# Softplus of a router: Ln on ScalarE against a series on VectorE, with a new order of all engines

## The reference

```python
logits = jnp.einsum('btd,ed->bte', X, routing_W) + expert_bias
activation = jnp.sqrt(jax.nn.softplus(logits))
top_vals, top_idx = jax.lax.top_k(activation, K)      # K = 2 of E = 8
combine = jnp.sum(jax.nn.one_hot(top_idx, E) * top_vals[..., None], axis=-2)
...
routed = jnp.einsum('ne,end->nd', cf, y)              # cf: combine, y: the experts' outputs
```

## Time and profile before

| | us |
|---|---|
| three runs | 233.58, 234.48, 235.31 |
| median | 234.48 |
| profiled execution | 234.76 |
| its span, first to last instruction | 233.0 |
| mean granted TensorE clock | 0.993 |

### The profile page before, as it was taken

One profiled execution on the slowest core, in us unless ns is written; L12 is line 12 of the kernel. 1 busy time (PEld: TensorE's weight loads), 2 busy tenths in 40 slices (PEclk: granted clock), 3 DMA queues, 4 the chain that ended last, 5 costly groups with the idle time before them and its releaser, 6 DMA issues.

```text
span 233.0 us, 5313 instructions
## 1 busy us (share of the span) xinstructions
PE 222.0 (95%) x2010; PEld 158.9 (68%) x2010; DVE 175.5 (75%) x507; ACT 132.9 (57%) x292; POOL 34.7 (15%) x55
## 2 busy tenths in 40 slices
PE   7999899999999999789899999999999989899995
PEld 6422685657786797455567766767677788798495
DVE  2476544999974699998887789999889767735672
ACT  2204462346377456889998888799987731133030
POOL 2020001032214126302040230020001031210000
PEclk9999999999999999999998999999999999999999
DMA  6999959600000000007000430000007999300001
GB/s 198 402 422 450 421 236 228 136 0 0 0 4 0 3 0 1 0 17 166 3 0 4 104 82 0 3 3 1 3 3 264 429 408 414 159 0 3 0 3 45
DMA packets 2905, 26.88 MB, mean 115 GB/s; under 512 B 448, under 2 KB 704, under 8 KB 1344
## 3 DMA queue, kind: packets, MB, share of 16 engines
q1 hardware_dynamic: 2880, 26.54, 31.5%
HBM read 26.28 MB, written 0.26 MB: 114 GB/s over the span
## 4 chain that ended last, share of the span: by engine, by line
PE 72%; DVE 10%; DMA 9%; ACT 3%; issue 2%; SPq 2%; POOL 0%; DVEq 0%
PE bank L1419 11%; DMA late_sb<-late 9%; PE bank L1435 6%; PE bank L1295 6%; PE bank L1405 5%; PE bank L1238 4%; PE bank L1234 3%; PE bank L1273 3%; DVE ctx_sb L954 2%; PE bank L1218 2%; PE bank L1378 2%; PE bank L1649 2%; PE bank L1361 2%; PE bank L1537 2%; PE bank L1640 2%
## 5 line engine op out<-in xcount | busy, mean ns | idle before, releaser
L579 ACT ACTIVATE ctx_sb<-ctx_sb,small_sb 128x512 f32<-128x512 f32 x64 | 45.9, 720 | 3.0 <-DVE small_sb L954 2.7
L954 DVE CUSTOM_DVE_ANT_0 ctx_sb<-bank,mask_sb 128x512 f32<-128x512 f32 x64 | 41.9, 679 | 2.6 <-PE bank L1419 1.8
L1419 PE MATMUL bank<-early_sb,ctx_sb 128*128 128x128 f32 x256 | 36.6, 281 | 2.3 <-DVE work_sb L965 1.4
L1419 PEld LDWEIGHTS bank<-early_sb,ctx_sb 128*128 128x128 f32 x256 | 28.3, 142 | 15.2 <-ACT ctx_sb L579 8.3
L381 POOL TENSOR_TENSOR rstd_sb<-veps_sb,minus_half_sb 128x2 f32<-128x2 f32 (+1 forms) x15 | 11.0, 733 | 129.9 <-DVE veps_sb L674 129.9
L590 ACT COPY work_sb<-bank 128x512 f32<-128x512 f32 x40 | 22.8, 579 | 8.1 <-PE bank L1419 7.7
L1405 PE MATMUL bank<-k_sb,work_sb 32*128 32x512 f32 x128 | 18.2, 638 | 1.3 <-DVE small_sb L954 1.1
L722 DVE SCALAR_TENSOR_TENSOR work_sb<-bank,early_sb,work_sb 128x512 f32<-128x512 f32 x16 | 11.8, 747 | 8.3 <-PE bank L1273 7.9
L1238 PEld LDWEIGHTS bank<-late_sb,ctx_sb 128*128 128x128 f32 x128 | 15.4, 191 | 3.4 <-issue 3.3
L1435 PE MATMUL bank<-work_sb,v_sb 128*32 128x128 f32 x512 | 17.3, 275 | 0.0
L965 DVE COPY work_sb<-bank 128x512 f32<-128x512 f32 x24 | 16.4, 682 | 0.8 <-PE bank L1419 0.8
(11 more groups left out here) (264 smaller groups left out, 398.4 us busy)
## 6 DMA issues: line engine op xcount, KB each, us to landing
k_sb<-moe_w SPq DMA_DIRECT2D x1, 4096.0 KB, 12.4
ctx_sb<-moe_w SPq DMA_DIRECT2D x1, 4096.0 KB, 17.1
ctx_sb<-ctx SPq DMA_DIRECT2D x3, 1024.0 KB, 14.7
late_sb<-late SPq DMA_DIRECT2D x1, 2966.5 KB, 21.1
mask_sb<-ctx_tok SPq DMA_DIRECT2D x1, 2048.0 KB, 13.2
v_sb<-ctx_tok SPq DMA_DIRECT2D x1, 2048.0 KB, 27.1
mask_sb<-mask SPq DMA_DIRECT2D x4, 512.0 KB, 7.8
mask_sb<-mask SPq DMA_DIRECT2D x8, 256.0 KB, 4.4
```

What stands on the lines that cost most here:

```text
L579: s.activation(sc[u % NSC], sc[u % NSC], ACT.Exp, bias=smin[:, u:u + 1], scale=-1.0, accum_out=rsum[:, u:u + 1]).then_inc(sig("p1_ready"), 1)
L954: v.tensor_tensor_reduce(sc[u % NSC], bank[SB[u % GROUPS]][:, :], mask[:, KEYS * b:KEYS * (b + 1)], MASK_BIG, 3e38, ALU.add, ALU.min, smin ...
L1419: last = nc.tensor.transpose(bank[TB[u % 2]][:, P * k:P * (k + 1)], sc[u % NSC][:, P * k:P * (k + 1)], wt("ident"))
```

## The change

Softplus is computed as max(x, 0) + 2 atanh(e / (2 + e)), since ln(1 + e) = 2 atanh(e/(2+e)). With ratio r = e/(2+e), at most 1/3, and r squared, the series r (1 + r2/3 + r4/5 + ... + r16/17) is evaluated from the inside out on DVE. ACT's Ln, its wait and its signal go, and so does the test for w = 1. The number of yields in the block on DVE stays 9; on ACT it is one less per half. The strings of all four engines are new. The new line is longer in letters as each stream is called three times more often than before in the string, which adds empty calls; the set of real steps is otherwise the same, apart from G, 39 before and 34 after.

```diff
--- before.py
+++ after.py
@@ -67,25 +67,26 @@
 
 TURNS = {
     "PE": (
-        "L2 P L11 P5 L P L8 P L2 a L2 P L a P L a3 L P L P L3 P6 a P L P2 L2 a L2 a P L2 a L2 a L a P a b P "
-        "a4 b P2 b P b a P a P2 S P2 S T5 S T V b T3 S T2 V T b2 S T3 b T S b V2 b T b S b T2 P b T b2 T S T2 "
-        "V T b T b T2 V S T3 V T2 S T V c T2 S T2 c T V T2 S T2 V T S c T P T c T2 V T c S T a T V c T2 c S "
-        "T2 c T2 c V T2 c S c b T2 V T V S T c T2 c V d c d2 G T G3 c d2 G d L2 d G3 a G d2 c G d c d G9 V G2 "
-        "b G d c d G d4 G3 d G3 d c G d G d G d G V G3 c G3 d6 S d5 T d10 "),
+        "L P L P L11 P5 L P L11 a L2 P L2 a L2 a3 P L P2 L P6 L a P L P L P L a L a L2 P a L2 a L a P2 b a3 L "
+        "a2 b P2 b P2 a b a P2 S P2 T S T2 S T3 a2 b T2 V T S T b a T b V T b T S T b T2 V T S b V T2 P b S b "
+        "T2 b3 T S T2 V b T2 b T V T S T2 V T2 S T2 V T L c T2 S T c b T V T2 S T c T V S T2 c a T2 V a c T2 "
+        "S V c T2 c T2 c T S T2 c V S T c T c S T L T V T2 V c T2 L c V d c V d2 c d2 G b V d2 G d2 G S G2 d "
+        "G3 d c2 G6 d c d G d3 c G d G2 V G T S T G d V G c T G d G d2 G b G3 d G P G P G c G3 b G d9 P d2 S "
+        "d2 V c2 d S d L d7 T d2 T b P "),
     "DVE": (
-        "L18 a L a L4 a L3 a4 L a L2 a4 L a4 L a2 L2 a4 L2 a3 L a L2 P a3 L a L2 a L b L2 P a5 L a2 b a3 L a5 "
-        "P a2 b P a b3 a b a2 b a b a b2 P a b4 P a2 b2 P b S4 b2 P b S2 T b L S2 b2 S b T S b S2 b T b2 S T "
-        "S b S2 b2 S b2 T b S3 b5 S2 b T b2 a S b2 V S b4 S V T S2 V S b2 P T b2 V S b S T S b2 S T c S3 T c "
-        "S c2 T c S3 V b S V T V2 c S2 T S c S c2 T c2 S4 T c2 S T S c S c S T c S2 T S c V S c V2 S T V c S "
-        "T S c S c2 T S2 c3 S c S T c V d V d b T d2 V d V2 P V3 d8 c2 d2 c S d c d5 S c d6 c3 L d c9 V c d14 "
-        "T d4 c d7 c d3 V d3 a d2 T d8 "),
+        "L21 a L a L4 a L a3 L a L a L2 a10 L2 a3 L a L a2 L3 a2 P L a2 L a2 L P L a L2 a4 b a L b L a5 P a5 "
+        "b2 a2 P a2 b3 a2 b a b2 a b P a b P b2 a b a L b2 P b S4 b2 P S3 b S b T b L b a S b T S b3 S b S T "
+        "b a S3 T b2 S b5 T b S b S b S b2 S b2 T S2 b V P V S2 a b2 V T b2 S4 V T b4 S2 b T S2 b2 T c3 S2 T "
+        "S2 c2 T S2 T S b V S V3 T c S3 c4 S T c2 S4 T c T S2 c2 S2 c T S3 P c V T c S V2 T c V S L S3 c T c "
+        "S c T S c S c3 S2 T c a V P d3 P T V d2 V a V5 d b d4 T d3 c d c2 d3 L d T d2 c d b P d V c T d5 c2 "
+        "L c d V c9 d2 S2 V d3 S d5 T c d6 b c d3 V d S b d4 c2 d2 V d2 c d5 c T d11 "),
     "ACT": (
-        "L2 P2 L P4 a L8 P2 L a2 P a2 P a P a2 P3 L P4 L2 a L2 a2 L a L a2 L2 a2 P L2 a P b P b2 a P b2 P b2 "
-        "S P S3 P T S T2 S3 T S T S T S3 a T S b T S2 b3 T S b2 S2 T b3 a T S T S3 T S4 T2 L S b T S4 T2 S2 "
-        "T2 S2 T S T S2 T S T S T S3 T S T S c T S2 T S2 T S c b c3 S T S T2 S3 T2 S4 T S T2 S3 T c T S c4 P "
-        "c d c S d c b d5 c T2 d6 c d4 "),
+        "L2 P3 L P4 a L P L8 a3 P2 a4 P4 L P3 L P L a L2 a2 L2 a2 L2 a P a L a P b P b2 a P b4 P S P S T S T "
+        "S4 T S T2 S L S2 T S b T S2 b2 T S b S b T S b S T b L S2 T b T S2 L S2 T S3 T2 S2 b T S3 T b T2 S2 "
+        "T S T S2 P T S T S a P S2 T2 S2 T S3 P T c b S P T S2 a T2 S2 c T c2 b c S3 P T2 S b T S T S4 T S T2 "
+        "S2 T b S c S2 a T2 c3 L T c L S c T a d c d c T c2 d5 S c d3 c d a d S d7 T c d "),
     "POOL": (
-        "L a L a4 b a L a2 b a3 b a b10 c2 L b c d c d a c d a c d2 c d2 ")}
+        "a L2 a6 b a L b a3 b2 a b7 a2 b c3 L3 b2 a d a c d c d2 b2 c2 d3 b d L c d2 a c2 ")}
 
 
 
@@ -554,9 +555,6 @@
                 act.wait_ge(sig("abs_ready"), h + 1)
                 s.activation(fr[2], fr[1], ACT.Exp, scale=-1.0).then_inc(sig("e_ready"), 1)
                 yield
-                act.wait_ge(sig("w_ready"), h + 1)
-                s.activation(fr[4], fr[3], ACT.Ln).then_inc(sig("ln_ready"), 1)
-                yield
                 hidden(4, B[0:H0, HTOK:], 1)
                 yield
                 for n in range(4):
@@ -859,7 +857,7 @@
                 normalize(h, x3, tiles)
                 yield
                 e3 = lambda a: a.rearrange("p (t e) -> p t e", e=E0)
-                logit, mag, ex, wl, lw, sp, av, t0, t1, cf = fr
+                logit, mag, ex, ratio, square, sp, av, t0, t1, cf = fr
                 if h:
                     dve.wait_ge(sig("cfT_ps"), 1)
                 dve.wait_ge(sig("route_ps"), h + 1)
@@ -869,29 +867,36 @@
                 ch.join()
                 v.scalar_tensor_tensor(mag, logit, -1.0, logit, ALU.mult, ALU.max).then_inc(sig("abs_ready"), 1)
                 yield
+                ch.add(v.tensor_scalar(sp, logit, 0.0, None, ALU.max))
                 dve.wait_ge(sig("e_ready"), h + 1)
-                v.tensor_scalar(wl, ex, 1.0, None, ALU.add).then_inc(sig("w_ready"), 1)
-                yield
-                dve.wait_ge(sig("w_ready"), h + 1)
-
-                ch.add(v.tensor_scalar(t0, wl, -1.0, 1e-30, ALU.add, ALU.max))
+                ch.add(v.tensor_scalar(t0, ex, 2.0, None, ALU.add))
                 yield
                 ch.join()
                 ch.add(v.reciprocal(t0, t0))
                 yield
                 ch.join()
-                ch.add(v.scalar_tensor_tensor(t1, wl, 1.0, ex, ALU.is_equal, ALU.mult))
-                ch.add(v.tensor_tensor(t0, t0, ex, ALU.mult))
-                yield
-                ch.join()
-                dve.wait_ge(sig("ln_ready"), h + 1)
-                ch.add(v.tensor_tensor(t0, t0, lw, ALU.mult))
-                yield
-                ch.join()
-                ch.add(v.tensor_tensor(t0, t0, t1, ALU.add))
-                yield
-                ch.join()
-                v.scalar_tensor_tensor(sp, logit, 0.0, t0, ALU.max, ALU.add).then_inc(sig("softplus_ready"), 1)
+                ch.add(v.tensor_tensor(ratio, ex, t0, ALU.mult))
+                ch.join()
+                ch.add(v.tensor_tensor(square, ratio, ratio, ALU.mult))
+                yield
+                ch.join()
+                ch.add(v.tensor_scalar(t0, square, 1.0 / 17, None, ALU.mult))
+                for n in (15, 13):
+                    ch.join()
+                    ch.add(v.scalar_tensor_tensor(t0, t0, 1.0 / n, square, ALU.add, ALU.mult))
+                yield
+                for n in (11, 9, 7):
+                    ch.join()
+                    ch.add(v.scalar_tensor_tensor(t0, t0, 1.0 / n, square, ALU.add, ALU.mult))
+                yield
+                for n in (5, 3):
+                    ch.join()
+                    ch.add(v.scalar_tensor_tensor(t0, t0, 1.0 / n, square, ALU.add, ALU.mult))
+                yield
+                ch.join()
+                ch.add(v.scalar_tensor_tensor(t0, t0, 1.0, ratio, ALU.add, ALU.mult))
+                ch.join()
+                v.scalar_tensor_tensor(sp, t0, 2.0, sp, ALU.mult, ALU.add).then_inc(sig("softplus_ready"), 1)
                 yield
                 dve.wait_ge(sig("softplus_ready"), h + 1)
```

## The result

The changed kernel takes 237.07 us (median of 12 runs, 235.84 to 241.82) where the kernel before, in the same comparison, takes 234.26: ratio 1.0117, 95% interval 1.0084 to 1.0150. Medians are over all executions, while ratios and intervals leave out those over 1.5% above the kernel's fastest (here 241.55 and 241.82 of the changed one). The prediction was 233.1, at most 235.3. It was wrong in sign.

A forecast was written before the change was run, and what follows sets the result against it. PE, busy 222.0 of 233.0 us, was taken as the bound, so its holes decide. 234.76 - 0.7 (start) + 0.3 (first half) - 1.0 (second half) + 0 (tail) = 233.4; less 0.28, 233.1 us, range 230.7 to 235.3.

The forecast's parts named there:

- The rows on ACT and DVE: Busy times: ACT loses 3 table loads and 2 Ln, 4.3 us; DVE gains 14 instructions of 0.17, to near 177.9.
- The start, -0.7: Widenings on DVE ahead of the first small-stage step close PE's 0.75 hole before 27.56: -0.7 us, ends -1.3 and 0.
- only a wait for the DMA would be a new hole, 0 to 0.5: At the start, PE's first projection, now ahead of the first transposes, may wait 0 to 0.5 us for ctx.
- First half, +0.3: Softplus near 67 comes 2.1 us later, with 1.7 of cover ahead of L1353: +0.3 us, ends 0 and +1.0.
- Second half, -1.0: Softplus near 113: an earlier router start pays for the series and PE's 0.96 of holes closes; ends -1.5 and +1.5.
- the router did not start 1.8 to 2.4 sooner: Second half: with two score turns and a copy less ahead on DVE, the router was to start 1.8 to 2.4 us sooner.
- softplus did not come 2 us ahead of 116: Sign of being right: softplus of the second half about 2 us before 116.
- The rival's row of eleven instructions: Second half, DVE from reciprocal to the next copy: PE loses 2.3 us instead of 0.73, in the 237.4 case, chance 0.14.
- Tail, 0: Behind the end of attention: five fillers fewer gain nothing; 0 us, ends -0.5 and +0.5.
- The clock, one fall as before: PE's clock falls once, as at 125 to 130; rival that it stays up: 1.7 us less, 231.4, chance 0.26.
- The rival "slower": Second half: PE waits behind DVE's row, +1.6, and a second clock fall adds +1.7: 237.4 us, chance 0.14.

The follow-up runs named there:

- giving the loads back: Series in the old order with one dummy Ln put back on ACT, so its table loads return, against the kernel before: 236.68 us, ratio 1.0124.
- the old first half: Series with the old order up to near 78 us and the new order behind it, against the kernel before: 235.39 us, ratio 1.0044.
- Covering the first wait: Changed kernel with PE's and ACT's old start, plus one projection moved ahead of L1358, against the kernel before: 234.81 us, ratio 1.0018.
- the moved turns: Old order with turns moved against the waits found; with the series, against the kernel before: 238.25 us, ratio 1.0057.
- the joined order: Full series, old order with hole-closing moves up to the middle of the first half's small stages, then new order, against the kernel before: 232.95 us, 0.9964.
- the kernel with the old head: Changed kernel with PE's and ACT's strings of before up to the end of local attention's first part, against the kernel before: 235.54 us, ratio 1.0037.
- the kernel with Ln and moved turns: Kernel before, Ln kept, two widenings moved ahead of the first small step and one thin-product copy ahead of step b33: 232.58 us, ratio 0.9944.

## Why the prediction was wrong

*The rows on ACT and DVE*: ACT's were right in size (4.4 us less). DVE's rise was 3.3 where 2.4 was forecast; with the series in the old order it is 2.6 (178.1), and the new order with Ln has 0.9 (176.4). It was right to count ACT's as beside the path: giving the loads back changed nothing in the old order. In the new order, with Ln, PE waited 2.1 us for ACT behind them.

*The start, -0.7*: the first step that failed. The hole at 26.8 did close, and alone that is worth 0.4% (0.9957), 1.0 us, with an interval that holds the forecast 0.7. But "only a wait for the DMA would be a new hole, 0 to 0.5" came true (0.41), and one wait was not looked for at all: the eighth projection, which covered ACT's L514 at 34.98, had been moved away, and 0.68 opened at 35.64. Undoing the head of PE and ACT gives 1.8 us back. With the 0.28 at 59.5, PE's idle time up to 90 went up by 0.90, where -0.4 was forecast with the first half's +0.3.

*First half, +0.3*: measured 0.41 at L1358, with 4.4 us from the Exp's end to softplus (68.39 to 72.81) where 4.5 was forecast, and no wait there in the new order with Ln. Right.

*Second half, -1.0*: -0.92 in the window 110 to 120. Right in number, and half by the reason given. From the Exp's end to softplus it took 4.2 us (114.38 to 118.55) where 4.3 was forecast. But the router did not start 1.8 to 2.4 sooner, and softplus did not come 2 us ahead of 116. The sum had left out what the changed kernel loses earlier. With the old first half, whose holes up to there are 0.9 us longer than before's, DVE's first router step stands at 110.72 against 110.76: the new second half is worth 0.9 of an earlier start. With the series in the old order a copy behind the chain makes PE wait 1.43; in the new order no such wait is there. The rival's row of eleven instructions did not become PE's wait in the changed kernel; in the old order its like did.

*The stretch from 120 to the tail*, counted at nothing, has +0.74 of idle time, most of it in three waits of 0.17, 0.26 and 0.35 for DVE. The same three stand in the new order with Ln (at 128.40, 145.47 and 160.75), so they belong to the order and not to the series. The forecast took the order behind 120 for neutral without following it.

*Tail, 0*: 49.30 to 49.28. Right.

*The clock, one fall as before*: the second step that failed, and the largest, by one fall, 1.72 in the profiled pair and about 1.6 on average. The forecast treated its fall as a property of the one stretch from 125 to 130 and asked only whether it would vanish. In the profile it did vanish, and two others came, one of them some 5 us behind the very wait that the forecast had written down as +0.3, the other right behind the hole of 1.62. Covering the first wait took its fall out of the profile and 0.5 of a fall off the average, which is no more than a hint at these numbers of runs; what sets the falls is open. The forecast also called the stretch ahead of its fall the busiest; by the earlier trace rows the busiest is the one from 27.56 to 90, with 0.13 of holes in 62.44, and it had no fall.

Taken together, in the profiled pair: of the 3.8 us between -1.4 and +2.4, 1.7 are the clock, 1.3 the holes up to 90, 0.7 those behind 120. The rival "slower" stood at 237.4, near the measured 237.07, but its mechanism and its place were wrong; only its second clock fall was right in number. That the chance of slower was put at 0.12 came from taking the new order's unknown terms as bounded by rows of holes, with no term for a hole's effect on the clock.

## What to carry to other kernels

When work moves to an engine that is full in the stretch, whoever is queued behind it pays, all of it in one order (1.6 us with the moved turns) and next to nothing in another (the joined order); the engine relieved pays back only where it was the releaser of a wait. When an order is rewritten, look at each piece of PE work that was moved and ask what it covered, the far ones too; and time a change of code in an order made for it, or part of what is measured is the order. Count clock falls run by run before comparing medians: a fall costs more than most waits do.

## What the runs showed of the hardware

The number of clock falls changes from one execution of a program to the next (61, 43 and 17 of 121 executions before with none, one and two), each worth 1.5 to 1.7 us. In the profiles its place goes with the order in part: at 80 to 86 and 98 to 106 with the new one, at 124 to 136 and in the tail with the old. One execution of the kernel with the old head took 357.98 us at a mean granted clock of 0.558. PE was busy in every us of the fall at 82 to 84 (2.00 of 2.00), as in the earlier trace rows. The Trainium skill (TensorE: Matmul & The Clock Gate, What's actually happening) has lack of activity set the throttle. The falls right behind the hole of 1.62 us in four of seven profiles would fit it; an execution with holes of 1.51, 1.09 and 1.43 us and a mean clock of 0.999 shows that a hole alone does not bring one, and the fall in the earlier trace rows stands behind 9 us without a hole over 0.15.

A dummy Ln of one element brought two table loads of 1.28, its own and the one back to Exp, and the instruction behind each started 1.29 to 1.30 after the load did. So did the instruction behind every load in every profile, but for one in the kernel with Ln and moved turns, which waited for DVE (1.74). No pause of the load's own was seen.
